# Two additions of running sums take one operand from PSUM in a feature-crossing kernel

## The reference, cut to what matters

```python
e = jnp.stack([tbl_0[ids[:, 0]], ..., tbl_38[ids[:, 38]]], axis=1)   # (1024, 39, 16)
x0 = xk = e
for W in [f0, f1, f2]:            # (39*39, 128), (128*39, 128), (128*39, 128)
    z = jnp.einsum('bfd,bgd->bfgd', x0, xk).reshape(b, f * g, d)
    cur = jnp.einsum('bpd,pm->bmd', z, W)
    outs.append(cur)
    xk = cur
z = jnp.sum(jnp.concatenate(outs, axis=1), axis=-1)                  # (1024, 384)
h = jnp.concatenate([z, dense_ctx], axis=1)
h = relu(h @ W_top1 + b_top1); h = relu(h @ W_top2 + b_top2); y = h @ W_top3
```

## Time and profile before

| | us |
|---|---|
| median of the three runs | 1470.94 |
| lowest and highest | 1468.39, 1472.05 |
| the profiled execution | 1473.32 |
| its span, first to last instruction | 1471.3 |
| PE busy | 1346.2 (92% of the span) |
| DVE busy | 1227.9 (83%) |
| ACT busy | 906.6 (62%) |
| POOL busy | 706.9 (48%) |

### The profile page before, as it was taken

The page is one execution under the profiler, slowest core; times in us unless marked ns, Lnnn a source line. Parts: engine busy times, 40 slices in busy tenths (PEclk is TensorE's granted clock), DMA queues, the critical chain, the costliest instruction groups (busy, mean ns, idle before and its releaser), DMA issues.

```text
span 1471.3 us, 20072 instructions
## 1 busy us (share of the span) xinstructions
PE 1346.2 (92%) x5856; PEld 996.8 (68%) x5856; DVE 1227.9 (83%) x2792; ACT 906.6 (62%) x3233; POOL 706.9 (48%) x697
## 2 busy tenths in 40 slices
PE   0188999999999999999999999999999998988998
PEld 0156666767777776777777776777777676766677
DVE  0268999998979899899989999799989989788874
ACT  1146676667666666666666676566666665655563
POOL 6686456654545466554545556454556523123200
PEclk9999999999999999999999999999999999999999
DMA  4171021100311021110211012110211002010000
GB/s 99 39 207 41 12 66 47 47 26 3 97 35 36 17 66 47 33 39 3 86 30 43 26 42 66 39 36 5 76 37 47 25 1 94 21 38 24 1 1 1
DMA packets 51355, 62.47 MB, mean 42 GB/s; under 512 B 12707, under 2 KB 24725, under 8 KB 51245
## 3 DMA queue, kind: packets, MB, share of 16 engines
q1 hardware_dynamic: 33644, 54.64, 12.1%
q0 software_dynamic: 10128, 2.98, 1.7%
q10 hardware_dynamic: 7473, 3.56, 1.0%
HBM read 10.02 MB, written 0.00 MB: 7 GB/s over the span
## 4 chain that ended last, share of the span: by engine, by line
PE 71%; DVE 16%; ACT 6%; issue 5%; ACTq 2%; DVEq 0%; DMA 0%
PE Y L735 17%; PE Y L737 15%; PE Y L736 15%; PE C L683 9%; PE C L697 5%; ACT Y L464 5%; PE S L691 5%; DVE cur L627 4%; DVE Y L624 3%; DVE sum_b L603 3%; DVE sum_a L603 2%; ACTq L232 2%; DVE part L616 1%; PE C L715 1%; PE C L706 1%
## 5 line engine op out<-in xcount | busy, mean ns | idle before, releaser
L464 ACT ACTIVATE Y<-Y,x_col 128x128 f32<-128x128 f32 x2944 | 800.1, 358 | 473.6 <-PE Y L737 455.1
L735 PE MATMUL Y<-f_high,cur_high 128*128 128x512 f32 (+1 forms) x1280 | 632.0, 494 | 54.5 <-DVE cur L627 37.4
L737 PE MATMUL Y<-f_high,cur_low 128*128 128x512 f32 (+1 forms) x1280 | 503.0, 393 | 0.0
L736 PE MATMUL Y<-f_low,cur_high 128*128 128x512 f32 (+1 forms) x1280 | 502.1, 392 | 0.0
L366 POOL TENSOR_TENSOR pairs<-shifted,base 117x512 f32<-117x512 f32 x186 | 240.3, 1294 | 531.4 <-PE C L683 529.5
L735 PEld LDWEIGHTS Y<-f_high,cur_high 128*128 128x128 f32 x1280 | 243.7, 190 | 198.0 <-DVE cur L627 76.9
L603 DVE SCALAR_TENSOR_TENSOR sum_a<-Y,x_col,sum_a 128x128 f32<-128x128 f32 x1024 | 349.9, 342 | 13.9 <-PE Y L737 0.5
L328 POOL DMA_INDIRECT rows<-in_tbl_dram,ids_sb x312 | 306.0, 981 | 83.0 <-issue 64.4
L603 DVE SCALAR_TENSOR_TENSOR sum_b<-Y,x_col,sum_b 128x128 f32<-128x128 f32 x896 | 305.5, 341 | 0.5 <-DVE sum_a L603 0.4
L736 PEld LDWEIGHTS Y<-f_low,cur_high 128*128 128x128 f32 x1280 | 244.9, 191 | 85.4 <-issue 47.8
L737 PEld LDWEIGHTS Y<-f_high,cur_low 128*128 128x128 f32 x1280 | 243.0, 190 | 52.2
(11 more groups left out here) (76 smaller groups left out, 568.0 us busy)
## 6 DMA issues: line engine op xcount, KB each, us to landing
shifted<-x_seq SPq DMA_DIRECT2D x157, 234.0 KB
base<-x_seq SPq DMA_DIRECT2D x95, 78.0 KB
rows<-in_tbl_dram,ids_sb POOLq DMA_INDIRECT x312
shifted<-x_seq SPq DMA_DIRECT2D x31, 156.0 KB
G<-in_L_rec_f_dram ACTq DMA_DIRECT2D x3, 832.0 KB, 6.4
w_sb<-in_W_top_dram SPq DMA_DIRECT2D x1, 768.0 KB
w_sb<-in_W_top_dram SPq DMA_DIRECT2D x1, 512.0 KB
shifted<-x_seq ACTq DMA_DIRECT2D x2, 234.0 KB
```

Source lines behind the costliest of these rows:

```text
L464: ins = act.activation(where[:, i * M:(i + 1) * M], where[:, i * M:(i + 1) * M], ACT.Copy, scale=x_col[:, t // JT % QG, t % JT, f:f + 1])
L735: pe.matmul(where, ch, wh, start=True, stop=False)
L736: pe.matmul(where, ch, wl, start=False, stop=False)
L737: pe.matmul(where, cl, wh, start=False, stop=True).then_inc(y_filled, 1)
```

## The change

It has three parts.

1. R1 writes its result, the part, not into SBUF but into the first 128 columns of chunk 3's bank, which DVE has already read. JOIN then adds one operand in PSUM and one in SBUF.
2. The last field that is added into `sum_b` (chunk 7, third field, `LAST_B`) writes its result over its own product in PSUM, and MERGE adds that and `sum_a`.
3. Since these banks are now read once more, two entries of `FREED` move: that of chunk 3 from step 9 (FUSE3 + 3) to step 11 (JOIN), and that of chunk 7 from step 19 (FUSE7 + 3) to step 20 (MERGE). So chunk 9 of a tile waits for JOIN of its own tile, and chunk 3 of the next tile for MERGE.

No instruction on any engine is added, dropped or moved; four per tile on DVE have other operands, and PE's two waits have other values.

```diff
-FREED = {0: R0, 1: R0, 2: FUSE2 + 3, 3: FUSE3 + 3, 4: R1, 5: R1, 6: FUSE6 + 3, 7: FUSE7 + 3, 8: R2, 9: R2}
+LAST_B = (7, 2)
+FREED = {0: R0, 1: R0, 2: FUSE2 + 3, 3: JOIN, 4: R1, 5: R1, 6: FUSE6 + 3, 7: MERGE, 8: R2, 9: R2}
...
-                        dve.scalar_tensor_tensor(acc, src, x, acc, ALU.mult, ALU.add).then_inc(acc_steps, 1)
+                        to = src if (c, i) == LAST_B else acc
+                        dve.scalar_tensor_tensor(to, src, x, acc, ALU.mult, ALU.add).then_inc(acc_steps, 1)
...
-                dve.tensor_reduce(part[:, t % 2, :], unit(t, 2), AX.X, ALU.add).then_inc(acc_steps, 1)
+                part = bank(t, 3)[:, 0:M]
+                dve.tensor_reduce(part, unit(t, 2), AX.X, ALU.add).then_inc(acc_steps, 1)
                 dve.wait_ge(acc_steps, n0 + R1)
-                dve.tensor_tensor(sum_a[:, t % 2, :], sum_a[:, t % 2, :], part[:, t % 2, :], ALU.add)\
-                   .then_inc(acc_steps, 1)
+                dve.tensor_tensor(sum_a[:, t % 2, :], part, sum_a[:, t % 2, :], ALU.add).then_inc(acc_steps, 1)
...
-                dve.tensor_tensor(bank(t, 9)[:, SUM_SLOT * M:], sum_a[:, t % 2, :], sum_b[:, t % 2, :], ALU.add)\
-                   .then_inc(acc_steps, 1)
+                c, i = LAST_B
+                dve.tensor_tensor(bank(t, 9)[:, SUM_SLOT * M:], bank(t, c)[:, i * M:(i + 1) * M], sum_a[:, t % 2, :],
+                                  ALU.add).then_inc(acc_steps, 1)
...
-            pe.wait_ge(acc_steps, NST * t + FUSE7 + 3)
+            pe.wait_ge(acc_steps, NST * t + MERGE)
```

More of the change, by code:

```diff
@@ L169, in build @@
         sum_b = sb("sum_b", [P, 2, M])
-        part = sb("part", [P, 2, M])
         cur1 = sb("cur1", [P, 2, M])
```

## The result

The changed kernel takes **1518.7 us** (median, 1510.8 to 1519.7); the kernel before takes 1471.5 beside it. The ratio is 1.031, with a 95% interval from 1.027 to 1.035. The forecast was slower, 1484 us, with a range up to 1508. The direction was right, the size was not: +47 us where +13 was forecast.

What follows compares the result with a forecast made beforehand. It took the loop around PE, ACT and DVE as the bound, with PE leading. Longer loops less removed standstill gave +9, waits +4: 1473.3 + 13 = 1486, forecast as 1484 us at the median; range 1446 to 1508.

Steps and rivals of the forecast that it cites:

- The operands: JOIN and MERGE on DVE: with one PSUM operand, 97 us of standstill leave and each addition takes 0.29 us.
- The moved wait: Chunk 9 waits for JOIN, so chunk 9, the layer2 slice and the addition go onto the loop: 1.8 us more at position 0.
- The sum: Tiles 20 to 99 +22 us, tiles 100 to 127 -12, first 20 about -1: +9, and +4 for waits.
- The walk: Loop from JOIN's end to the next, per position (tile in a group of four): 11.2, 10.0, 10.0, 10.6 us.
- irregular waits: Idle time ahead of MERGE on DVE, beyond its own start and waits for ACT, carried by half: +4 us.
- The covered wait: PE reaches chunk 9 after JOIN, so the moved wait is free: 1400 us; chance 0.09 for under 1446.
- half way: ACT and PE run closer together, 0.3 us less on each of 128 loops: 1446 us; chance 0.09 for 1446 to 1466.
- the standstill that stays: Additions are caught whatever their operands, DVE keeps 97 us and PE gets new waits: 1550 us; over 1508 shared 0.08.
- The loop is dearer: Each 0.1 us more per loop, from longer release or slower matmul starts, costs 13 us; over 1508 shared 0.08.

Runs made afterwards that it cites:

- the kernel that keeps PE busy: Changed kernel with chunk 8's three matmuls repeated three times more at position 3 of each group, while PE waits for JOIN: 1493.1 us, ratio 1.014.
- the second half alone: Kernel before with only the last field of sum_b in PSUM and chunk 3 waiting for MERGE; chunk 9 free: 1426.5 us beside 1460.1, ratio 0.977.
- the kernel with the moved slice: Changed kernel with the first layer2 slice of 21 groups moved ahead of chunk 9 of the tile before: 1481.7 us beside 1460.1, ratio 1.013.
- the late join with the wait: Against the kernel before: part in SBUF, both additions behind chunk 7 with one PSUM operand, chunk 9 waiting for R1: 1487.0 us beside 1460.1, ratio 1.019.
- the kernel with the waits alone: Kernel before with its SBUF operands, but chunk 9 waiting for JOIN and chunk 3 for MERGE: 1571.5 us, ratio 1.068.

## Why the prediction went wrong, point by point

**The operands.** Right. 97 us of standstill were forecast to leave and did: the means fell from 704 to 291 and from 640 to 300 ns, which is 128 x (413 + 340) ns = 96 us. Additions of 0.29 and 0.30 us were forecast and measured.

**The moved wait.** Right, to within 0.2 us per tile. Forecast per position 11.2, 10.0, 10.0, 10.6; measured at full clock 11.2, 10.0, 10.0, 10.8. With the MLP 15.6 was forecast, and 15.6 measured. With transposes the group was to take 43.2, and takes 43.3 in the kernel that keeps PE busy. "At positions 0 and 3 it is early by 0.8 and over 2 us" came out as 0.7 and 2.0 us of idle time. The wait of chunk 3 for MERGE cost nothing in the changed kernel, as forecast: no matmul waited for it. Where the loops are shorter, in the second half alone, it bit by 8.0 us.

**The sum.** The walk gave 866.5 and 301.6 us for the two stretches; with the clock held up they are 871.7 and 303.9. That is 7.5 us over the walk, where the forecast had added 4 for irregular waits. The forecast of -1 us for the first 20 tiles was about right: tiles 1 to 19 take 193.6 us with the clock held up, and took 195.4 before.

**The step that failed** is the last sentence of the prediction: "The clock plays no part unless PE's granted clock falls in a stretch with these waits." All its prices were taken at full clock, and it forecast 2 us of PE idle time at position 3 of 32 groups without asking what such a pause does to the clock. The trace of before had the warning already. There PE pauses for over 1.4 us only some dozen times after 100 us, mostly behind a long standstill of DVE, and each of its eight falls between 100 us and the tail begins behind such a pause, of 1.75 to 3.84 us, or up to 1.0 us before the end of the pause. One of them, by windows:

```profile
1295.00:1299.00 4.00, 0.18 (x1) 0.00 (x0) 3.96 (x3) 0.00 (x0) 2.55 (x3) 0.90 0.33 100
1299.00:1303.00 4.00, 3.98 (x9) 3.00 (x10) 3.26 (x9) 1.12 (x4) 0.00 (x0) 0.50 0.00 0
```

The change trades these rare pauses for 31 regular ones. The mechanism of the loops was right, and one term was put at nothing without a reason: a fall behind the pause costs 1.6 us in a group without the MLP (12.8 for 11.2) and 4.2 to 5.8 with it (19.9 to 21.4 for 15.6), where the fall lasts longer and the MLP's matmuls run on PE inside it. Over the 108 tiles that makes 22.6 + 9.0 = 32 us. 1484 + 32 = 1516, against 1518.7 measured. That it comes so close is in part luck: the 32 us are the difference of two single executions, and the medians with the clock held up differ by only 25. The executions differ too: those of the changed kernel lie between 1510.8 us, at a mean clock of 0.977, and 1519.7, at 0.955.

**The rivals.** The covered wait, half way and the standstill that stays are all out: chunk 9's wait is one for one on the loop, and no addition was caught. "The loop is dearer" had the right sign, but put it down to each loop. What was dearer was one loop in four, the one behind position 3, and of these only about half. It had 0.08 together with the standstill.

**The chances.** Slower had 0.68 and happened; the range ended 11 us short. A regular pause that PE had only rarely before was a reason for a longer upper side.

## What to carry to other kernels

When a buffer gets one more reader, look up who waits for it to be free, and what is queued behind that wait; a change of one step in such a table cost 6% here, while the gain that it was to allow was 4% and could be had without it. The distance around the loop, walked from rows and once for each kind of tile, predicted such a change to within 0.2 us per tile, as long as the clock stayed up. But check what new pauses it gives PE, and price the work behind the longest of them also at the lower clock.

## What the runs showed of the hardware

**PE's clock fell behind some pauses of 1.5 to 2 us.** The changed kernel idles PE for about 2.0 us at position 3 of a group (1.6 in the third of a block). Behind 15 of its 24 pauses of 2.0 us or more, the granted clock was at 0.5, from 0.2 us before the end of the pause to 2.0 us after it: for 3.4 us in the eleven without the MLP, for 10.2 to 13.7 us in the four with it. Behind its seven pauses of 1.6 us, and of 0.9 in the kernel with the moved slice, it never fell. But 1.6 us is no bound. In the late join with the wait the pauses are 1.7 us long, and nine falls stand behind them; one, by its row and a window:

```profile
743.66 0.45 PE L738 MATMUL Y<-f_high,cur_high 128*128 128x384 f32 x1 [1.69 <-DVE part L619]
```
```profile
745.00:749.00 4.00, 4.00 (x15) 3.52 (x16) 2.40 (x6) 0.57 (x3) 0.00 (x0) 0.50 0.01 3
```

In the kernel with the waits alone, falls stand behind pauses of 1.5 us too. So the length of the pause does not decide by itself, and what does stays open. In the changed kernel 2.1 us of repeated matmuls in the pause removed all these falls and paid for themselves. Why the falls last longer with the MLP was not tried.

**An addition with two SBUF operands can be held by more than one POOL instruction.** In the kernel before, JOIN of tile 73 starts while POOL issues a gather that ends at 858.66, and it is not through before the pair behind that has ended too (timeline rows):

```profile
857.71 0.95 POOL L328 DMA_INDIRECT rows<-in_tbl_dram,ids_sb  x1 [0.30 <-issue]
...
858.01 2.12 DVE L618 TENSOR_TENSOR sum_a<-sum_a,part 128x128 f32<-128x128 f32 x1
...
858.67 1.30 POOL L366 TENSOR_TENSOR pairs<-shifted,base 117x512 f32<-117x512 f32 x1
```

The same pattern, 2.09 to 2.12 us long, stands in twelve JOINs. The gather by itself does not hold an addition. Nine other JOINs and one MERGE start about as far into a gather, with 0.6 to 0.7 us of it to go, and take 0.29 to 0.30 us; what differs is that POOL's next instruction comes 0.3 us or more behind the gather, and in the twelve a pair stands 0.01 to 0.02 us behind it. One of the ten:

```profile
984.17 0.94 POOL L328 DMA_INDIRECT rows<-in_tbl_dram,ids_sb  x1 [0.30 <-issue]
984.50 0.29 DVE L618 TENSOR_TENSOR sum_a<-sum_a,part 128x128 f32<-128x128 f32 x1
...
986.49 1.26 POOL L342 COPY rows_seq<-rows 128x624 f32<-128x624 f32 x1 [1.37 <-DMA rows<-in_tbl_dram,ids_sb]
```

Why a pair holds an addition that, by the rows, started 0.65 us before it is open. The Trainium skill (SBUF — State Buffer, Who interferes with whom) has the loser wait for one instruction. Here an addition could lose to several that came back to back: the MERGE of the earlier trace rows ends only behind four spreads and a pair, and the longest JOIN, of 5.1 us, behind two spreads and three pairs.
